# Gate and up products of a pair's two experts in the two halves of the array's rows, with weights in runs of 3072 bytes

## The reference

```python
# x: 8192 tokens of 256 features; 64 experts, the 8 best for each token, at most 128 tokens per expert
g = jnp.einsum('ecd,edf->ecf', xb, w_gate)      # 64 x (128 x 256) @ (256 x 192)
u = jnp.einsum('ecd,edf->ecf', xb, w_up)
h = jax.nn.silu(g) * u
y = jnp.einsum('ecf,efd->ecd', h, w_down)       # 64 x (128 x 192) @ (192 x 256)
routed = segment_sum(weight * y over each token's experts)
out = routed + shared expert
```

## Time and profile before

| | |
|---|---|
| median of 3 runs | 2587.45 us (2583.96 to 2590.21) |
| profiled execution: time, span | 2582.3 us, 2580.6 us |
| busy share of the span | PE 93%, DVE 64%, ACT 53%, POOL 45% |
| expert stage of the first mixture | about 1352 to 1587 us |
| expert stage of the second mixture | about 2339 to 2581 us, the end of the kernel |

### The profile page before, as it was taken

One profiled execution on the slowest core, in us unless ns is written; L12 is line 12 of the kernel. 1 busy time (PEld: TensorE's weight loads), 2 busy tenths in 40 slices (PEclk: granted clock), 3 DMA queues, 4 the chain that ended last, 5 costly groups with the idle time before them and its releaser, 6 DMA issues. The chain is left out here.

```text
span 2580.6 us, 48369 instructions
## 1 busy us (share of the span) xinstructions
PE 2395.2 (93%) x14822; PEld 1295.1 (50%) x14822; DVE 1651.4 (64%) x3745; ACT 1366.6 (53%) x2766; POOL 1150.1 (45%) x1497
## 2 busy tenths in 40 slices
PE   7997999999999999979998996899999969997997
PEld 4664233333333333356556664566666646555765
DVE  6777888888888888446552322688888746553321
ACT  4666677767766776646522322455555427632322
POOL 6998111111111011123326775677777724324776
PEclk9998799999999999989999998999999989998999
DMA  5655423232333232136767874011111026585886
GB/s 172 204 194 173 124 84 100 86 101 84 97 87 99 86 96 64 37 123 201 244 212 195 231 196 75 16 37 38 38 38 34 20 75 204 194 279 159 228 206 110
DMA packets 286870, 325.20 MB, mean 126 GB/s; under 512 B 30496, under 2 KB 272368, under 8 KB 286704
## 3 DMA queue, kind: packets, MB, share of 16 engines
q1 hardware_dynamic: 252928, 274.22, 33.9%
q0 software_dynamic: 29184, 46.43, 9.0%
q10 hardware_dynamic: 4592, 2.47, 0.4%
HBM read 217.29 MB, written 105.19 MB: 125 GB/s over the span
## 5 line engine op out<-in xcount | busy, mean ns | idle before, releaser
L716 DVE TENSOR_REDUCE a_row_max<-a_ps_m 128x2 f32<-128x1024 f32 x512 | 607.4, 1219 | 84.6 <-PE a_ps_m L619 79.6
L776 ACT ACTIVATE a_probs<-a_ps_s 128x512 f32<-128x512 f32 x1024 | 536.8, 602 | 206.9 <-PE a_ps_s L647 206.6
L662 PE MATMUL a_ps_o<-a_probs,a_va 128*32 128x512 f32 x2048 | 274.1, 608 | 0.8 <-ACT a_o_sb L785 0.8
L1738 POOL TENSOR_TENSOR b_spread<-b_decay,held_own_sb 128x512 f32<-128x512 f32 x256 | 269.0, 1082 | 8.2 <-DVE b_weight L1799 8.2
L1799 DVE TENSOR_TENSOR b_weight<-b_ps_s,b_spread 128x512 f32<-128x512 f32 x256 | 163.7, 681 | 17.6 <-PE b_ps_s L1939 17.6
L647 PE MATMUL a_ps_s<-first_qs,first_ks 98*128 98x512 bf16 (+1 forms) x512 | 161.0, 396 | 3.1 <-DMA first_qs<-a_m_parts 3.1
L647 PE MATMUL a_ps_s<-second 98*128 98x512 bf16 (+1 forms) x512 | 157.0, 387 | 4.4 <-DMA second<-a_m_parts 2.3
L556 POOL CAST a_high<-a_row_max 128x32 bf16<-128x32 f32 x32 | 6.5, 204 | 316.2 <-DVE a_row_max L716 316.2
L597 POOL DMA_DIRECT2D x<-a_xo x32 | 24.2, 755 | 275.3 <-DVE a_xo L750 272.9
L1558 DVE SCALAR_TENSOR_TENSOR m2e_h<-m2e_act_g,m2e_xg,m2e_ps_h 128x192 f32<-128x192 f32 x64 | 26.5, 414 | 150.7 <-ACT m2e_act_g L1487 132.9
L315 PE MATMUL a_ps_qk<-a_w_qk,a_xnT 128*128 128x512 f32 x256 | 122.6, 602 | 0.0
(11 more groups left out here) (381 smaller groups left out, 5389.6 us busy)
## 6 DMA issues: line engine op xcount, KB each, us to landing
parts<-second SPq DMA_DIRECT2D x16, 1536.0 KB, 6.2
second<-parts SPq DMA_DIRECT2D x384, 64.0 KB
rows<-m_early SPq DMA_DIRECT2D x32, 640.0 KB
m_early<-x SPq DMA_DIRECT2D x31, 512.0 KB
first_qs<-parts SPq DMA_DIRECT2D x192, 64.0 KB, 2.7
first_ks<-parts SPq DMA_DIRECT2D x192, 64.0 KB, 2.3
m_own<-in_L_ffn_w_gate_dram SPq DMA_DIRECT2D x24, 384.0 KB, 6.8
m_own<-in_L_ffn_w_up_dram SPq DMA_DIRECT2D x24, 384.0 KB, 7.0
```

The lines of the kernel that those rows point to most:

```text
L662: last = nc.tensor.matmul(ps_o[VW * j:VW * (j + 1), :], va[n.u][:, t, (h0 + j) * VW:(h0 + j + 1) * VW], probs[:, group % 2, j, t, :], star ...
L716: nc.vector.tensor_reduce(row_max[:, n.k // 4 % 2, t, :, n.p % 4], m_bank(name, step)[:], AX.X, ALU.max).then_inc(m_drained, 1)
L776: nc.scalar.activation(probs[:, group % 2, j, t, :], s_bank(name, step)[:], ACT.Exp, scale=DK ** -0.5).then_inc(s_drained, 1)
L1738: nc.gpsimd.tensor_tensor(spread[:, n % 2, heads].rearrange("p h t c -> p (h t) c"), decay[:, n % 3, heads].rearrange("p h (t o) -> p (h t ...
```

## The change

The turned x no longer has one expert after the other, each over all 128 rows. Feature 4p+c of the first expert's tokens is now in row p, that of the second's in row 64+p, for c = 0 to 3. The weights of gate and up lie in the same way, so the run that a row reads from HBM has four features of 192 numbers, 3072 bytes, where there were two runs of 1536 bytes, one per expert. Gate and up are then 8 products over 64 rows, alternating between the halves and the two banks, where there were 4 over 128 rows. To bring x into halves, `turn` is no longer four transposes but eight ordinary products with the unit matrix, each of which writes 64 rows of `ps_x`. Both experts' gate and up products are now one stage ahead of `add_shared`, and `h_ready` rises once for a pair.

```diff
@@ pair_of_weights
-        yield gate_up[:, :, m], w[two].rearrange("e (p c) f -> p e c f", c=2)
+        yield gate_up[:, m], w[two].rearrange("e (p c) f -> (e p) c f", c=4)
@@ moe_experts
-        xgT = sb("xgT", [P, 2, 2, C, P])
+        xgT = sb("xgT", [P, 2, CX, P])
@@ turn, on TensorE
-                for j in range(2):
-                    for c in range(C):
-                        last = nc.tensor.transpose(ps_x[:, j, c, :], xg[:, i % XB, j, c:D:C], ident[:])
+
+                for c in range(CX):
+                    for j in range(2):
+                        last = nc.tensor.matmul(ps_x[HALF * j:HALF * (j + 1), c, :], xg[:, i % XB, j, c:D:CX], ident[:], start=True, stop=True)
                 last.then_inc(x_turned, 1)
@@ gate_up, on TensorE
-            def gate_up(j):
-                def stage(i):
-                    if j == 0:
-                        wait(pe, w_loaded[i % WB], 48 * (i // WB))
-                        pe.wait_ge(xT_done, i + 1)
-                    wait(pe, h_done, 2 * (i - 1) + j + 1)
-                    for c in range(C):
-                        last = nc.tensor.matmul(ps_h[j][:], xgT[:, i % 2, j, c, :], w_gu[i % WB][:, j, :, c, :], start=c == 0, stop=c == C - 1)
-                    last.then_inc(h_ready, 1)
-                return stage
+            def gate_up(i):
+                wait(pe, w_loaded[i % WB], 48 * (i // WB))
+                pe.wait_ge(xT_done, i + 1)
+                wait(pe, h_done, 2 * i)
+                for c in range(CX):
+                    for j in range(2):
+                        rows = slice(HALF * j, HALF * (j + 1))
+                        last = nc.tensor.matmul(ps_h[j][:], xgT[rows, i % 2, c, :], w_gu[i % WB][rows, :, c, :], start=c == 0, stop=c == CX - 1)
+                last.then_inc(h_ready, 1)
@@
-            in_turn([(L_SAME, spread_first), (L_TURN, turn), (L_DOWN, down_both), (L_GU, gate_up(0)), (L_DOWN, add_shared), (L_GU, gate_up(1)),
-                     (L_TURN_H, turn_h)])
+            in_turn([(L_SAME, spread_first), (L_TURN, turn), (L_DOWN, down_both), (L_GU, gate_up), (L_DOWN, add_shared), (L_TURN_H, turn_h)])
@@ ScalarE
-                wait(act, h_ready, 2 * (i - 1))
+                wait(act, h_ready, i - 1)
...
-                    act.wait_ge(h_ready, 2 * i + j + 1)
+                    act.wait_ge(h_ready, i + 1)
```

More of the change, by code:

```diff
@@ L1290, in moe_experts @@
     P, D, T, E, F = 128, 256, 8192, 64, 192
-    PAIRS, C = E // 2, 2
-    CD = 2 * F // P
+    PAIRS = E // 2
+    CD, CX = 2 * F // P, 2 * D // P
     HALF = P // 2
@@ L1326, in moe_experts @@
         ps_r = pb("ps_r", [P, P])
-        ps_x = pb("ps_x", [P, 2, C, P])
+        ps_x = pb("ps_x", [P, CX, P])
         ps_h = [pb(f"ps_h{j}", [P, 2, F]) for j in range(2)]
-        ps_t = pb("ps_t", [P, 2, C, P])
+        ps_t = pb("ps_t", [P, CX, P])
         ps_y0 = [pb(f"ps_y0{u}", [P, D]) for u in range(2)]
@@ L1350, in turned_h @@
         def turned_h(c):
-            return ps_t[:].rearrange("p a b q -> p (a b q)")[:, c * P:(c + 1) * P]
+            return ps_t[:, c, :]
         def in_turn(stages):
@@ L1462, in turn_b_weights @@
                 wait(pe, w_copied, i - 1)
-                bank = (ps_x, ps_t)[i % 2]
+                bank = (ps_x, ps_t)[i % 2][:].rearrange("p (c r) q -> p c r q", c=2)
                 for c in range(2):
@@ L1492, in copy_h @@
                 wait(act, y0_ready, i - 1)
-                nc.scalar.activation(hT[:, i % 2].rearrange("p c q -> p (c q)"), ps_t[:].rearrange("p a b q -> p (a b q)")[:, 0:CD * P], ACT.Copy).then_inc(hT_done, 1)
+                nc.scalar.activation(hT[:, i % 2].rearrange("p c q -> p (c q)"), ps_t[:, 0:CD, :].rearrange("p c q -> p (c q)"), ACT.Copy).then_inc(hT_done, 1)
             def copy_second(i):
@@ L1503, in keep_b_weights @@
                 act.wait_ge(w_turned, i + 1)
-                bank = (ps_x, ps_t)[i % 2]
+                bank = (ps_x, ps_t)[i % 2][:].rearrange("p (c r) q -> p c r q", c=2)
                 if i < 3:
-                    nc.scalar.activation(b_w[i][:].rearrange("p (c a) -> p c a", c=2), bank[:].rearrange("p c r a -> p c (r a)"), ACT.Copy).then_inc(w_copied, 1)
+                    nc.scalar.activation(b_w[i][:].rearrange("p (c a) -> p c a", c=2), bank.rearrange("p c r a -> p c (r a)"), ACT.Copy).then_inc(w_copied, 1)
                 elif i == 3:
-                    nc.scalar.activation(b_w[3][:].rearrange("p (c a) -> p c a", c=2)[:, :, 0:D], bank[:].rearrange("p c r a -> p c (r a)"),
+                    nc.scalar.activation(b_w[3][:].rearrange("p (c a) -> p c a", c=2)[:, :, 0:D], bank.rearrange("p c r a -> p c (r a)"),
                                          ACT.Copy).then_inc(w_copied, 1)
@@ L2061, in mixture @@
                     down = ahead_x[:, 0:DOWN] if memory is own and k == 0 else memory[:, at + GU:at + GU + DOWN]
-                    buffers.append((memory[:, at:at + GU].rearrange("p (j m c f) -> p j m c f", j=2, m=2, c=2),
+                    buffers.append((memory[:, at:at + GU].rearrange("p (m c f) -> p m c f", m=2, c=4),
                                     down.rearrange("p (c d) -> p c d", d=D)))
```

## The result

| | before | changed |
|---|---|---|
| median of 4 runs each | 2585.7 us (2583.68 to 2590.21) | 2609.61 us (2605.36 to 2611.55) |
| ratio, with its 95% interval | 1 | 1.0097, 1.0076 to 1.0118 |
| profiled execution: time, span | 2582.3 us, 2580.6 us | 2611.55 us, 2609.9 us |

The changed kernel is 23.9 us slower, where the forecast was +7.2. The time lies inside the stated range of 2580 to 2616. In a second comparison (experiment 5) the same kernel was 17.2 us slower, 1.0070 [1.0043, 1.0096].

The account below looks back on a forecast made before the run. It took TensorE to bound the first half of an expert stage and GpSimd the second. First mixture +5.7 us and second +1.5, together +7.2 on 2587.45, gave 2594.7 us; range 2580 to 2616.

Parts of the forecast that it names:

- What bounds the kernel, and the waits: Expert stages: TensorE at 6.8 us a pair becomes slower than GpSimd needs, gather waits go, nothing waits in steady state.
- Gate and up products, 2.60: TensorE step: 16 half records take 2.60 us where 8 whole ones took 2.58, +0.02.
- Turning, 0.86: TensorE step: 16 records of 128 columns on 64 array columns take 0.86 us instead of 0.45, +0.41.
- One more change of the array, +0.21: TensorE step: three switches between whole array and halves, or between kinds of halves, instead of two; +0.21 us, bounds 0 and 0.42.
- Start, +2 us: Start of an expert stage: slower first turning and later hidden values start TensorE 2 us later.
- the 4 us that the prediction named as a sign of being wrong: Expert stage start: a start more than 4 us later would show the prediction wrong.
- The first scatter, put at +3.1: Expert stage start: GpSimd's first scatter comes 3.1 us later, from 2 and half a stage's 1.3; bounds 0 and 4.
- Sum: Both expert stages: last scatter 5.7 us later in the first mixture, +1.5 in the second, together +7.2 us.
- Loads: Gate and up weight loads: half as many packets save 0.35 us of each DMA engine per pair, shortening nothing directly.
- the rival on the fast side: Expert stages: a shorter DMA queue removes much of GpSimd's waits, step at most 6.55 us, kernel 2580; chance 0.17.
- GpSimd staying the bound: Expert stages: a step of 6.6 to 6.7 us hides in GpSimd's pace, no difference, 2585 to 2590; chance 0.16.
- Small products cost more than their columns: Turning: records come every 0.08 us instead of 0.054, step 7.2 us, kernel +29, 2616; chance 0.08.

Follow-up runs that it names:

- experiment 5: The changed kernel run again, not edited, against the kernel before in its own group: ratio 1.0070 [1.0043, 1.0096].
- experiment 7: Changed kernel, but from pair 1 on each turning product moves 64 columns instead of 128 (half the tokens); ratio to the kernel before 1.0068.
- experiment 6: Changed kernel, but each turning product loads 64 columns lying side by side instead of every fourth one; ratio to the kernel before 1.0046.
- experiment 1: Kernel before with only the gate and up weights loaded in runs of 3072 bytes; ratio to the kernel before 1.0013.
- experiment 2: Kernel before with only both experts' gate and up products merged into one stage ahead of add_shared; ratio to the kernel before 1.0018.
- experiment 4: Changed kernel with four buffers for gathered rows instead of eight; ratio to the kernel before 1.0071.
- experiment 3: Kernel before with only the turning's four transposes replaced by eight products (16 records) with the unit matrix; ratio to the kernel before 1.0011.
- experiment 11: Kernel before with four buffers for gathered rows instead of eight; ratio to the kernel before 0.9990.
- experiment 10: Same kernel as experiment 1 (kernel before, weight runs of 3072 bytes), run again as a control with eight buffers; ratio to the kernel before 1.0021.
- experiment 9: Same kernel as experiment 4 (changed kernel, four buffers for gathered rows), run again in another group; ratio to the kernel before 1.0022.
- group 3: The runs of experiment 9, experiment 10 and experiment 11, compared with the kernel before run alongside; ratios 1.0022, 1.0021 and 0.9990.
- group 2: The runs of experiment 5, experiment 6, experiment 7 and the unedited kernel before, on the same chip as group 1; kernel before 2584.93 us.
- group 1: The runs of experiment 1, experiment 2, experiment 3 and experiment 4, compared with the kernel before run alongside at 2570.87 us.

## Why the prediction was right or wrong

**What bounds the kernel, and the waits:** right. The gather waits vanish, the step is the same to the end of the stage, and the last scatter begins 1.25 and 1.0 us behind the last copy.

**Gate and up products, 2.60:** right, 2.68 with the change behind them counted in. Halves of the rows cost nothing in themselves.

**Turning, 0.86:** too small. The weight loads of its 16 records take 1.04 us in the timeline of the same step; the other 0.13 I take for the change behind it. The estimate was worked out from moved columns; experiment 7 shows that the weight loads count, and experiment 6 that 0.15 of it is the distance between the columns. With columns up to two apart it is 1.02 - 0.13 = 0.89, the estimate.

**One more change of the array, +0.21:** too large. It shows as 0.10 ahead of the turning, 0.10 more in `add_shared` and 0.10 less in down: together +0.1. The two errors partly cancel, which is why the step, 6.81 forecast and 6.87 measured, looks better than its terms were.

**Start, +2 us:** this is the step that failed, in both stages. Against 28.2 and 28.1 it was +6.5 and +5.6, beyond the 4 us that the prediction named as a sign of being wrong. The first scatter, put at +3.1 (2 and 1.3 are 3.3), came 7.6 and 6.7 us later. Where there is no standstill, T4 goes from about 22 (experiments 1 and 2) to 23.5 (experiment 4), +1.5, near the forecast. The missing 4 to 5 us are ScalarE's standstill, which was in the trace of before, 5.07 us ended by "remote", and which I had taken for a part of the start that the change could not touch. In the changed kernel it catches `copy_x` of pair 1, on which both experts' gate and up of that pair wait, and then the first silu; before it caught only silus of pair 1. Whether the merged order or the turning by 16 records moves it there is not shown: experiments 2 and 3 ran only in the group without it, and the 0.15 us a step of experiment 6 left T4 at 34.5. That it ends with the burst of gathers is shown by experiment 11 against 10 in one group, and by experiment 9 against 5 across two. By what means the gathers and the late landings hold ScalarE up is not settled: no packet of the instruction queues lay in that time, and the trace names no event of the kernel's.

**Sum.** In the first stage, +6.5 (2) at the start, +9.3 (7.7) in 27 steps, -2.7 (-4.0) of backlog and +0.4 behind the last turning: +13.5, where +5.7 was forecast. In the second +5.6, +2.5 and +0.4, less 1.3: +7.2, where +1.5 was. Of the 13.5 us by which the two stages together were missed the start has 8.1 (4.5 and 3.6), the steps 3.2, and the smaller gain from GpSimd's backlog with the ends the rest. The difference between 20.7 and 23.9 is within what the untouched stages vary from one execution to the next. That the time stayed inside the stated range is in part luck: the upper part of the range was there for a rival with a step of 7.2 us, and no case had a start this late.

**Loads.** "0.35 us of each DMA engine per pair saved" rested on comparing two stretches with different work. Experiments 1 and 10 give nothing for it, so the rival on the fast side had no ground, and the Trainium skill (DMA: Bandwidth & Descriptors, Specifications) was the better guide: it puts the limit at 512 bytes, and from 1536 to 3072 bytes these runs show no gain. The lower DMA share came as forecast, but not from this cause: fewer bytes were moved in the same time.

**The other rivals.** GpSimd staying the bound nearly came true for experiment 3, whose step of 6.72 cost at most 0.3%, though no gather waits were left in it; the changed kernel lies 0.15 above it. "Small products cost more than their columns" was given 0.08 and was partly what happened: 0.065 us a record and not 0.08.

## What to carry to other kernels

Read the start of a stage row by row before pricing a change of its order, and look at every idle time that ends with nothing of the kernel's own: a wait that falls on a harmless instruction in one kernel fell on one that all else hangs on in the other. When an operand is loaded as weights with few moved columns behind it, price the load, with the distance between its elements, and not the columns. A saving of an engine that isn't the bound, and a burst that builds up a lead, are worth only what the bound lets through: in group 3 the changed kernel with four buffers is 0.2% slower than before, where with eight it was 0.7% slower in group 2, and the kernel before gains nothing by them.

## What the hardware showed that I had not expected

- Weight loads of 64 fp32 columns take 137 ns side by side, 138 two apart, 209 four apart. Transposes of 128 columns two apart take 207 and side by side 140 ns, so in them two apart already costs; why is open.
- ScalarE stands still while GpSimd issues indirect DMAs back to back, 8.0 + 3.7 us in the changed kernel and about 5 in the one before for 14 gathers of 1.25 us, 3.8 us and none for 8, in groups in which a load of 384 KB lands after about 6 us, and not where it lands after 4.3. The kernel before is 14 us faster in group 1 (2570.87 us), where loads land early, than in group 2 (2584.93 us), on the same chip. What makes the groups differ, and whether the late landings or something behind both holds ScalarE up, is open.
- From whole to half and back costs 0.08 to 0.13 us at a place, an estimate from the starts of the groups. The down products take 0.19 more than 12 x 0.1085 where a whole group follows (1.49 in the kernel before, and in experiment 3, where halves of the columns stand ahead of them), and 0.10 where halves of the rows follow (1.40). So what comes behind them makes that difference, and not what stands ahead.
